# A recurrent scan beside an FFN: each scan matmul streams tanh's two parts once instead of twice

## The reference, cut to what matters

```python
def _derivative(q, p, drive, coupling, bias):
    i_couple = jnp.tanh(q) @ coupling.T
    dq = q - q ** 3 / 3.0 - p + drive + i_couple + bias
    dp = EPSILON * (q + ALPHA - BETA * p)
    return (dq, dp)
# _rk4_step calls it four times, each on the result of the one before; lax.scan over 256 steps
gate_up = jnp.einsum('bsh,oh->bso', x, w_gu)
h = jax.nn.silu(gate) * up
y = jnp.einsum('bsi,hi->bsh', h, w_down)
rms = jnp.sqrt(jnp.mean(y * y, axis=-1, keepdims=True) + EPS)
# out = x + y / rms
```

## Time and profile before

| | us |
|---|---|
| median of 3 runs | 1520.15 |
| lowest and highest | 1519.74 and 1520.77 |
| the profiled execution | 1519.87 |
| its span in the trace | 1518.0 |

### The profile page before, as it was taken

How to read it: one execution, slowest core, us unless ns; L and a number is a source line. 1 busy time by engine, 2 the same in 40 slices (tenths; PEclk the granted TensorE clock), 3 DMA queues, 4 the chain that set the end, 5 groups by cost and what they waited for, 6 DMA issues and landing times.

```text
span 1518.0 us, 90291 instructions
## 1 busy us (share of the span) xinstructions
PE 1424.1 (94%) x36992; PEld 1408.7 (93%) x36992; DVE 1434.8 (95%) x10781; ACT 718.9 (47%) x4836; POOL 12.2 (1%) x38
## 2 busy tenths in 40 slices
PE   0277999999999999999999999999999999999998
PEld 0166999999999999999999999999999999999998
DVE  6999999999999999999999999999999999999991
ACT  2144445445454544545454454545445455544541
POOL 0000000000000000000000000000000000000000
PEclk9999999999999999999999999999999999999999
DMA  9500000000000000000000000000000000000000
GB/s 243 138 7 4 15 7 8 22 8 21 4 8 21 8 21 8 21 4 7 21 8 22 7 22 4 8 21 8 22 8 21 7 4 22 7 21 8 22 4 22
DMA packets 13520, 32.67 MB, mean 22 GB/s; under 512 B 1712, under 2 KB 6064, under 8 KB 12976
## 3 DMA queue, kind: packets, MB, share of 16 engines
q1 hardware_dynamic: 13104, 26.89, 6.7%
HBM read 22.69 MB, written 4.19 MB: 18 GB/s over the span
## 4 chain that ended last, share of the span: by engine, by line
PE 89%; DVE 5%; ACT 0%; issue 0%; POOLq 0%; DVEq 0%; POOL 0%; ACTq 0%
PE scan_ps L518 53%; PE gu_ps L295 22%; PE y_ps L307 14%; DVE th L590 1%; DVE q_stage L626 1%; DVE with_q L584 1%; DVE q_stage L628 1%; DVE q_sq L594 0%; DVE scan_ps L602 0%; DVE p_part L584 0%; DVE q_cub L597 0%; DVE with_p L584 0%; ACT th L556 0%; DVE q_raw L628 0%; DVE q_raw L626 0%
## 5 line engine op out<-in xcount | busy, mean ns | idle before, releaser
L518 PE MATMUL scan_ps<-th,wscan 128*128 128x32 f16 (+1 forms) x32768 | 1015.9, 175 | 87.6 <-ACT th L556 87.0
L518 PEld LDWEIGHTS scan_ps<-th,wscan 128*128 128x128 f16 x32768 | 937.9, 96 | 102.6 <-ACT th L556 95.1
L556 ACT ACTIVATE th<-q_stage 128x16 f16<-128x16 f32 x1536 | 318.5, 207 | 527.6 <-DVE q_stage L626 527.6
L295 PE MATMUL gu_ps<-hist,wffn 128*128 128x128 f32 x2816 | 503.3, 284 | 0.0
L295 PEld LDWEIGHTS gu_ps<-hist,wffn 128*128 128x128 f32 x2816 | 393.9, 192 | 0.0
L590 DVE TENSOR_TENSOR th<-t,th 128x16 f16<-128x16 f32 x2048 | 352.6, 172 | 1.1 <-ACT t L558 0.6
L307 PE MATMUL y_ps<-wffn,h 128*128 128x128 f32 x1408 | 323.6, 313 | 0.0
L558 ACT ACTIVATE t<-q_stage 128x16 f32<-128x16 f32 x1536 | 305.8, 199 | 0.0
L556 ACT ACTIVATE th<-q_raw 128x16 f16<-128x16 f32 x512 | 106.2, 207 | 220.8 <-DVE q_raw L626 182.6
L307 PEld LDWEIGHTS y_ps<-wffn,h 128*128 128x128 f32 x1408 | 209.5, 189 | 0.4 <-DVE h L323 0.4
L373 ACT ACTIVATE sum_r<-dr,constant 128x64 f32<-128x64 f32 x528 | 174.1, 332 | 7.8 <-DMA dr<-drive 7.8
(11 more groups left out here) (33 smaller groups left out, 539.3 us busy)
## 6 DMA issues: line engine op xcount, KB each, us to landing
raw<-packed SPq DMA_DIRECT2D x11, 768.0 KB, 9.0
dr<-drive SPq DMA_DIRECT2D x34, 128.0 KB, 2.5
sc<-scales SPq DMA_DIRECT2D x11, 384.0 KB, 9.3
xres<-x SPq DMA_DIRECT2D x16, 256.0 KB, 3.5
out<-osb SPq DMA_DIRECT2D x16, 256.0 KB, 2.9
coup<-coupling_t SPq DMA_DIRECT2D x1, 1024.0 KB, 15.0
q_raw<-cond_t SPq DMA_DIRECT2D x1, 16.0 KB, 1.6
bias<-bias_t SPq DMA_DIRECT2D x1, 2.0 KB, 1.7
```

Of the source, the lines that this page charges most:

```text
L295: i = nc.tensor.matmul(gu_ps[b][:, half * P:(half + 1) * P], wffn[:, u, j * P:(j + 1) * P], hist[1 - f.parity][:, kt].rearrange("p t b -> ...
L518: i = nc.tensor.matmul(to if both else to[:, 0], wscan[:, w, part, kt, cols], moving if both else moving[:, 0], start=first, stop=last, sk ...
L556: nc.scalar.activation(th[s % 2][:, c, 0, :], q[:, c, :], ACT.Tanh, scale=1.0 / S).then_inc(now.tanh_hi, 1)
```

## The change

COPIES goes from 2 to 1. The width of the slots that TensorE writes and the repeat of the streamed tanh both follow from it.

```diff
-COPIES = 2
+COPIES = 1
```

## The result

| | before | after |
|---|---|---|
| median, us | 1520.28 | 2034.66 |
| lowest and highest | 1519.74, 1520.77 | 2034.47, 2035.10 |
| the profiled execution, and its span | 1519.87, 1518.0 | 2034.47, 2032.7 |
| ratio, 95% interval | | 1.338 (1.336 to 1.341) |

A forecast was written before the change was run, and what follows sets the result against it. TensorE was taken to set the pace beside the FFN, VectorE in block 0. 1519.9 us, pace 0, +514 for the low clock, +2 in the tail, -1 latency in block 0 gave 2035 us; range 1517 to 2050.

The forecast's parts named there:

- What bounds the kernel: Beside the FFN, TensorE sets the pace with VectorE 2% behind; in block 0 it is the other way round.
- Pace: Scan matmuls: each costs some 26 ns with its weight load, so halving the columns gains 0 per stage.
- Whatever it streams, at either level: Scan matmuls: the fixed cost of some 26 ns each holds for any column count, at low and high clock.
- Latency: Reductions L626 and L628 wait for a half's last matmul, now shorter: 1.5 us gained, at most 7.5.
- In block 0 DVE itself is full: Block 0: VectorE is busy 72.8 of 75 us; given as a reason to take little of the 7.5 us bound.
- DVE hardly ever waits for PE: VectorE waited for the scan's sums only 8.2 us, 41 times; given as a reason for a small gain.
- Clock: TensorE beside the scan: the thinner stream may not raise the clock, 1.917 us a stage, +514 us; tail +2.
- the choice between the cases: TensorE's clock after the change: low all through 0.42 (2035 us), low for a part 0.28, as before 0.30.
- Low clock for a part: Rival: TensorE's clock comes up late or alternates, 0.54 us per low stage, 1563 to 1900 us; chance 0.28.
- Clock as before: Rival: only columns hidden under a fixed price go, 1518.4 us, between 1512.4 and 1520; chance 0.30.

The follow-up runs named there:

- copies3: The kernel before with three copies instead of two (48 and 24 columns, 1248 a stage): 1545.1 us, ratio 1.015; one of three executions took 2090.6 us.
- wide01: The changed kernel with two copies in blocks 0 and 1, one from block 2 on: 1515.1 us, ratio 0.997; two of eight executions took 1734.5 and 1733.1.
- last1b: The kernel of last1 measured once more, beside two kernels that build on it: 1514.92 us, ratio 0.9962 to the kernel before.
- last1: The kernel before, with one copy only in the last matmul of each half of the neurons (800 columns a stage): 1515.16 us, ratio 0.9957.
- zeros: The kernel before, with the second 8 columns of each pair taken from a part set to zero once: 1519.49 us, ratio 0.9985.
- twelve4: The changed kernel, with the twelve single matmuls streaming tanh's high part four times (704 columns a stage): 1516.91 us, ratio 0.9985.
- fill0: last1 with an extra matmul of 384 columns, result unread, in all 64 stages of block 0: 1513.60 us, ratio 0.9953 to the kernel before.
- prime: The changed kernel with a burst of 24 extra matmuls of 512 columns, result unread, between block 0 and block 1: 2038.97 us, ratio 1.342.
- prime_b2: The changed kernel with the burst of 24 matmuls of 512 columns before block 2, where stages have two FFN products: 1552.65 us, ratio 1.021.

## Why the prediction was right

**What bounds the kernel.** Right. TensorE sets a stage beside the FFN, so a slower TensorE lengthens it in full; VectorE's share went to 0.73 (foreseen 0.70), and its waits before L626 are (365.3 + 105.9) / (713 + 238) = 0.50 us each, as foreseen. The waits of the kernel after (us in total, times, longest):

```profile
DVE q_stage L626 <- PE scan_ps L518: 365.3, 713, 1.0
DVE q_raw L626 <- PE scan_ps L518: 105.9, 238, 0.5
```

**Pace.** Right: 0 gained, 0.90 us a group with 32 or with 16 columns. "Whatever it streams, at either level" was too wide: in copies3, at the low level, 48 columns cost 0.27 us more a group.

**Latency.** The mechanism was right, the size too small: 1.5 us forecast, in a bound of 7.5, and 4.0 (wide01), 5.7 (last1b) and 6.6 us (last1) measured, of which the stages of last1 account for 11 ns x 64 + 4 ns x 960 = 4.5. Two steps failed. "In block 0 DVE itself is full" was taken to mean that it gains nothing; a stage there went from 1.387 to 1.376 us, 11 of the 12 ns. And "DVE hardly ever waits for PE" was read from a row that can't show it. In these rows of DVE before, L628 starts at 702.48, just 0.04 us after the last matmul of the group that starts at 701.47 and lasts 0.97. L626 starts 0.05 us before the recorded end of L584. So an earlier instruction's 0.18 us lies over any wait, and it isn't counted as idle:

```profile
702.17 0.18 DVE L584 SCALAR_TENSOR_TENSOR with_q<-hist,with_p 128x32 f32<-128x32 f32 x1
702.30 0.21 DVE L626 TENSOR_REDUCE q_stage<-scan_ps 128x16 f32<-128x48 f32 x1
702.48 0.21 DVE L628 TENSOR_REDUCE q_stage<-scan_ps 128x16 f32<-128x48 f32 x1
```

A stage with two products went from 1.3648 to 1.3609 us in last1 (means of 658 and 660 stages), 4 of 7 ns. In the kernel after this gain is buried under the clock.

**Clock.** Right, term by term, once the case was chosen. From 154.24 to 1992.55 us there are 959 stages, 1838.3 us, 1.917 us each. The tail from the last stage's FFN to the end is 2032.7 - 1992.55 = 40.2 us against 1518.0 - 1479.52 = 38.5, +1.7 for +2. Block 0 gave back 155.27 - 154.24 = 1.0 us. L295 is at 428 ns, foreseen near 430.

**The weak step** was the choice between the cases, which no row settled; 0.42 was a lean, and that the time came out within 1 us of the forecast is luck in so far as this choice was. It rested on the low clock of block 0 in spite of TensorE's occupation there. The runs bear it out: zeros and twelve4 leave the pace and the number of the matmuls as they are and give the time back by columns alone. fill0 raises the clock without the FFN, though there the extra matmul adds columns and closes the idle time at once; that closed idle time isn't enough by itself is shown by the kernel after. The rule of the Trainium skill weighed in the prediction (page "TensorE: Matmul & The Clock Gate", section "HAM oscillation — how this bites in real kernels") doesn't cover this: from 166 to 2000 us in prime TensorE has no wait at all in the trace and stays at 0.50.

**The rivals.** "Low clock for a part" didn't occur in the kernel after, and the few executions of wide01 and copies3 at 0.78 show that a mixed case exists. Its counter-argument, that the higher level holds itself, is half true: with two products a stage it held (prime_b2, four executions of four), and where stages had one it fell (prime). "Clock as before" is refuted for this kernel. What lowered the clock in those executions, the stream or something from outside, stays open.

## What to carry to other kernels

Work that costs no time of its own may be paying for the clock. Before narrowing a matmul whose pace is fixed by its weight load, look at which level the clock has in each stretch (by the durations, as the clock's column can be blank) and at who else depends on it. If columns serve only to keep the clock, leave them out just where somebody waits for the matmul's end: that gave some 0.3 to 0.4% here, in ten executions of last1 and last1b that all kept the clock.

## What the runs showed of the hardware that was not expected

The clock has a memory in effect: one and the same stream stays at the low level for 1834 us if it starts there, and at the high level for 1190 us if a burst of 24 matmuls precedes it. Columns of zeros kept it as copies of tanh do (zeros). And one matmul in a stage can be enough to tip it: 384 columns behind 32 small matmuls made it alternate between both levels every few stages, with the time within 1.3 us of last1b.
